# Attention and a mixture of experts on one core: experts in fixed blocks of 128 slots, shared products last

## The reference, cut to what matters

```python
xn = layernorm(x)
# attention: 16 heads of 16
scores = (q @ k.T) * SCALE * decay * causal        # no softmax
y = layernorm(scores @ v, ln_w, ln_b)
attn = (y * silu(xn @ wg.T)) @ wo.T
# experts: E = 32, K = 4, I = 192
top_vals, top_idx = top_k(xn @ router_w.T + router_b, 4)
rw = softmax(top_vals) * 1.8
routed = sum_k rw[k] * (silu(xn @ gate[e].T) * (xn @ up[e].T)) @ down[e].T
shared = (silu(xn @ sg.T) * (xn @ su.T)) @ sd.T
out = x + attn + routed + shared
```

## Time and profile before

| | us |
|---|---|
| median of 3 runs | 325.85 |
| range of the runs | 322.96 to 326.37 |
| span of the profiled execution | 308.4 |
| TensorE busy in the span | 267.0 |
| VectorE, ScalarE, GpSimd busy | 146.2, 75.3, 145.3 |

### The profile page before, as it was taken

How to read it: one execution, slowest core, us unless ns; L and a number is a source line. 1 busy time by engine, 2 the same in 40 slices (tenths; PEclk the granted TensorE clock), 3 DMA queues, 4 the chain that set the end, 5 groups by cost and what they waited for, 6 DMA issues and landing times.

```text
span 308.4 us, 5576 instructions
## 1 busy us (share of the span) xinstructions
PE 267.0 (87%) x1522; PEld 180.7 (59%) x1523; DVE 146.2 (47%) x488; ACT 75.3 (24%) x217; POOL 145.3 (47%) x164
## 2 busy tenths in 40 slices
PE   6699989998699999999999999999999999993000
PEld 2577867876488877767555565555555555551000
DVE  2913988979435563734613233223232332321393
ACT  1031231111111111211223333323333233320230
POOL 0063060607306074604375667667666676433480
PEclk9799999999699999999999999999999999998555
DMA  6999950000000002000039998984212222111982
GB/s 199 391 353 426 425 108 2 0 0 1 2 1 2 1 2 68 2 0 19 18 89 248 291 299 271 288 281 159 73 55 84 66 90 80 52 36 44 332 261 85
DMA packets 16725, 40.13 MB, mean 130 GB/s; under 512 B 2934, under 2 KB 10555, under 8 KB 16065
## 3 DMA queue, kind: packets, MB, share of 16 engines
q1 hardware_dynamic: 12048, 29.43, 28.5%
q0 software_dynamic: 4224, 9.97, 10.2%
q10 hardware_dynamic: 432, 0.47, 0.7%
HBM read 33.57 MB, written 7.86 MB: 134 GB/s over the span
## 4 chain that ended last, share of the span: by engine, by line
PE 75%; DVE 13%; DMA 4%; POOL 3%; issue 2%; ACT 0%; SPq 0%; DVEq 0%; POOLq 0%
PE bank L1110 18%; PE bank L1134 9%; PE bank L1048 8%; PE bank L1132 6%; PE bank L1102 5%; PE bank L988 4%; DVE x_sb L880 4%; PE bank L956 4%; PE bank L972 3%; PE bank L1119 3%; PE bank L964 3%; PE bank L1082 3%; DVE w L763 2%; DMA w<-y_rows 2%; PE bank L1079 2%
## 5 line engine op out<-in xcount | busy, mean ns | idle before, releaser
L1110 PE MATMUL bank<-w,xbT 128*128 x176 | 64.5, 489 | 0.6 <-ACT xbT L449 0.4
L533 POOL DMA_INDIRECT y_rows<-loop_mem,sidx x44 | 44.5, 1012 | 34.4 <-issue 25.0
L526 POOL DMA_INDIRECT xg<-xn_rows,gidx x44 | 43.1, 981 | 18.2 <-issue 12.3
L817 DVE TENSOR_TENSOR state_mem<-loop_mem,bank 128x192 f32<-128x192 f32 x44 | 15.6, 354 | 62.6 <-ACT loop_mem L453 62.6
L1110 PEld LDWEIGHTS bank<-w,xbT 128*128 128x128 f32 x176 | 30.0, 190 | 13.0 <-issue 1.2
L1048 PEld LDWEIGHTS bank<-w 128*128 128x128 f32 x256 | 31.6, 198 | 2.3 <-issue 0.6
L1048 PE MATMUL bank<-w 128*128 128x128 f32 x256 | 32.3, 281 | 0.0
L1134 PE MATMUL bank<-w,loop_mem 64*128 x88 | 30.6, 428 | 0.0
L504 POOL TENSOR_SCALAR w<-w,cst 128x256 f32<-128x256 f32 x8 | 7.8, 973 | 45.4 <-ACT w L424 45.4
L449 ACT COPY xbT<-bank 128x256 f32<-128x256 f32 x44 | 16.3, 373 | 49.6 <-PE bank L1102 49.6
L824 DVE COPY loop_mem<-bank 128x256 f32<-128x256 f32 x44 | 18.7, 425 | 20.1 <-PE bank L1134 20.1
(11 more groups left out here) (145 smaller groups left out, 385.2 us busy)
## 6 DMA issues: line engine op xcount, KB each, us to landing
w<-w_exp_dram SPq DMA_DIRECT2D x17, 512.0 KB, 5.1
w<-w_exp_dram SPq DMA_DIRECT2D x3, 2560.0 KB, 16.4
w<-y_rows SPq DMA_DIRECT2D x8, 512.0 KB, 7.3
w<-w_exp_dram SPq DMA_DIRECT2D x1, 1088.0 KB, 7.9
x_sb<-x_dram SPq DMA_DIRECT2D x4, 256.0 KB, 5.7
w<-w_qkvg_dram SPq DMA_DIRECT2D x2, 512.0 KB, 7.7
w<-decay_dram SPq DMA_DIRECT2D x1, 1024.0 KB, 10.3
xn_rows<-w SPq DMA_DIRECT2D x2, 512.0 KB, 3.4
```

Of the source, the lines that this page charges most:

```text
L526: nc.gpsimd.indirect_dma_start(xg[:, u, :], None, xn_rows, bass.IndirectOffsetOnAxis(ap=gidx[:, u:u + 1], axis=0),).then_inc(tok_in[u], 16)
L533: nc.gpsimd.indirect_dma_start(y_rows, bass.IndirectOffsetOnAxis(ap=sidx[:, w:w + 1], axis=0), ysb[:, w, :], None, bounds_check=ROWS - 1, ...
L1110: last = nc.tensor.matmul(ps_gu[(u - 1) % 2][:, 0:2 * I], xbT[:, (u - 1) % 2, g * P:(g + 1) * P], w1[:, bass.ds(e_gu * EW + g * 2 * I, 2 * ...
```

## The change

What it does, part by part:

- **Experts.** Each expert has one fixed block of 128 slots, and two experts make a pair that is worked on together in 16 steps written out without a loop. The weights are the standing operand and the tokens stream, so that the hidden values come out with features on the partitions and are not transposed. The two 64-row halves of the hidden values of a pair lie one below the other. Tokens beyond 128 go to overflow blocks of four pieces of 32 slots, each piece with an expert of its own: four such blocks are always done, more only if needed (`later_rounds`). For a piece, ScalarE copies the expert's weights (1024 columns) to a fixed place, and a small DMA brings the rest.
- **Attention.** Scores are eight products of 256 columns in four row groups. Values are weighed by 16 products that each fill 32 columns of the array, four column groups in turn. Scores of a tile are no longer cut in halves. Tile 0 is loaded and normalised alone. The state is updated one tile later. The inverse root goes over a power on GpSimd and one refinement. The query masks move to ScalarE. The output's normalisation goes over ScalarE, VectorE and GpSimd. The routing's steps lie at other tiles (ranks at 2, inverse at 6), and its one-hot positions are made by ScalarE and GpSimd.
- **Shared expert.** It leaves the attention's tiles and is done after the experts, features on the partitions, in four groups of 256 tokens. The transposed tokens are written to memory and loaded back for this.
- **Tail.** `y_rows` is ordered by partition. VectorE adds the four rows for tiles 0 to 4 and two rows of tile 5, in an order that takes two tiles in turn. TensorE adds the other ten rows by products with diagonal matrices.
- **Weights.** 9 pairs are loaded early, 7 late.

The diff's core (`...` where lines are left out):

```diff
-            def scores(t, half):
...
-                for par, q in enumerate((qe, qo)):
-                    for g in range(KT):
-                        for b in range(2):
-                            rows = slice(32 * (2 * half + b), 32 * (2 * half + b + 1))
+            def scores(t):
...
+                for g in range(KT):
+                    for r in range(HG // 2):
+                        rows = slice(CT * r, CT * (r + 1))
+                        q = qeo[rows, t % 2, :].rearrange("p (a n) -> p a n", a=2)[:, :, g * P:(g + 1) * P]
+                        last = nc.tensor.matmul(ps_s[r][:, 2 * g * P:2 * (g + 1) * P],
+                                                qk[rows, t % 2, (KT + g) * P:(KT + g + 1) * P],
+                                                q, start=True, stop=True)
...
+            def weigh_values(t):
...
+                for g in range(KT):
+                    for par in range(2):
+                        for r in range(HG // 2):
+                            s = 4 * r + 2 * g + par
+                            h = head_of_slot(s)
+                            last = nc.tensor.matmul(ps_y[CT * r:CT * (r + 1), g * P:(g + 1) * P],
+                                                    vz[:, t % 2, h * CT:(h + 1) * CT], st[:, s * P:(s + 1) * P],
...
+            def transpose_pair(p):
...
+                for j in range(2):
+                    k = AT["P", 2 * p + j]
+                    for g in range(KT):
+                        last = nc.tensor.transpose(ps_xt[p % 2][:, (2 * g + j) * P:(2 * g + j + 1) * P],
+                                                   xg[:, k % RING, g * P:(g + 1) * P], ident)
...
+            def gate_up(n):
...
+                for m in range(3):
+                    for g in range(KT):
+                        o = j * EW + g * MB + m * P
+                        last = nc.tensor.matmul(ps_gu[j][:, m * P:(m + 1) * P], w[:, o:o + P],
+                                                xbT[:, p % 2, (2 * g + j) * P:(2 * g + j + 1) * P],
...
+            def down(p):
...
+                for j in range(2):
+                    nc.tensor.matmul(ps_dn[j][:, 0:D], hA[:, 2 * (p % 2) + j, :], w[:, j * EW + KT * MB:j * EW + XW],
+                                     start=True, stop=False)
+                for j in range(2):
+                    rows = slice(j * I2, (j + 1) * I2)
+                    nc.tensor.matmul(ps_dn[j][:, 0:D], hC[rows, p % 2, :], w2[rows],
+                                     start=False, stop=True).then_inc(dn_ps, 1)
...
+            def overflow_gate_up():
+                for g in range(KT):
+                    for j in range(SUBS):
+                        rows = slice(SUB * j, SUB * (j + 1))
+                        o = j * OW + g * MB
+                        last = nc.tensor.matmul(ps_og[rows, 0:MB], xbO[:, g * P + SUB * j:g * P + SUB * (j + 1)],
+                                                o_mem[:, o:o + MB], start=(g == 0), stop=(g == KT - 1),
...
+            def shared_gate_up(i):
...
+                for m, to in enumerate((ps_sa[i % 2][:, 0:2 * P], ps_sa[i % 2][:, 2 * P:4 * P], ps_sc[i % 2][:, 0:2 * P])):
+                    for g in range(KT):
+                        o = g * MB + m * P
+                        last = nc.tensor.matmul(to, ws_mem[:, o:o + P], xnT_back[:, g, n],
...
+            def output_scale(t):
...
+                pool.wait_ge(mo_sb, t + 1)
+                step(nc.gpsimd.tensor_tensor(yrstd[:, s], yvar[:, s], minus_half[:, 0:1], ALU.pow))
...
+            def copy_weights(i, j):
+                e = act.value_load(eid_row[0:1, bass.ds(i, 1)], min_val=0, max_val=E - 1)
+                return nc.scalar.copy(o_mem[:, j * OW:j * OW + XW], w_mem[:, bass.ds(e * EW, XW)])
...
+            def weigh_routed(n):
...
+                    last = nc.tensor.matmul(ps_sd[n // 2 % 2][n % 2][:, 0:D], diag[:, i, :], back[:, n, k, :],
+                                            start=False, stop=(k == TOPK - 1 or (i, k) == rows[-1]))
```

More of the change, by code:

```diff
@@ L58 @@
 C_GC = C_KD + H
[L59 to L60 removed]
+C_IO = C_GC + KT
 C_PI = C_IO + P
@@ L319, in states_before, with state_reads @@
             return sum(1 for u in range(t) if u % CPB < CPB - 1)
+        def state_reads(t):
+            return sum(1 for u in range(t + 1) if u % CPB > 0)
         def need(eng, semaphore, value):
@@ new lines, in take_logits_transposed, with hot_positions @@
+            def take_logits_transposed():
+                act.wait_ge(lgT_ps, 1)
+                nc.scalar.copy(lgT[:, :], ps_vg[:, 0:2 * P]).then_inc(lgT_sb, 1)
+            act_hot = [a for a in range(NA) if a not in POOL_HOT]
+            hot = [0]
+            def hot_positions(t, place):
+                for _ in range(HOT_STEPS.get((t, place), 0)):
+                    a = act_hot[hot[0]]
+                    if hot[0] == 0:
+                        act.wait_ge(pos_sb, 1)
+                    nc.scalar.activation(pos_hot[:, a, :], iota_bf[:, :], ACT.Abs, scale=-1.0, bias=pos_f[:, a:a + 1]
+                                         ).then_inc(abs_sb, 1)
+                    hot[0] += 1
@@ L586, in _ @@
+            for w in range(YRING):
+                pool.wait_ge(sent[w], 16 * SENT[w])
+            later_rounds(pool, later)
         @block.vector
@@ L1162, in _ @@
+            project_qk(1)
             for t in range(NT):
                 more = t + 1 < NT
-                scores(t, 0)
+                if t >= 1:
+                    scores(t)
+                if t == CPB + 1:
+                    transpose_keys(CPB)
+                if t == 1:
+                    router_logits()
+                if t == T_INVERT:
+                    route_inverse()
+                if not more:
+                    transpose_pair(0)
+                if t % CPB > 0 and t != CPB + 1:
+                    chunk_products(t - 1)
```

1740 lines of the change are left out of this document (1109 added, 631 removed).

## The result

The changed kernel takes **235.37 us** (median of 4 runs, 235.03 to 236.57), the kernel before 325.8 us (322.96 to 326.37) beside it: a ratio of 0.7234, 95% interval 0.7193 to 0.7274. The forecast was 250 with a range of 229 to 274, so the direction and the range held and the figure was 6% too high. The profiled execution has a span of 233.7 us and a time of 235.56.

| stage | predicted | after | after, where no release is late (below) |
|---|---|---|---|
| first scores start | 14 | 11.9 | 12.0 |
| attention ends | 100.5 | 85.1 | 81.8 |
| experts | 104.2 | 124.0 | 94.4 |
| tail | 28 | 24.6 | 24.6 |
| time above the span | 17.45 | 1.9 | 1.9 |

What follows compares the result with a forecast made beforehand. The prediction took the kernel as TensorE's work plus a tail without it. Attention to 100.5, experts 104.2 and tail 28 gave a span of 232.7 us; with 17.45 carried, 250, range 229 to 274.

Steps and rivals of the forecast that it cites:

- Tiled products, taken at 2.0 times: Scores, values and overflow blocks: four row or column groups of TensorE run 2.0 times as fast, bounds 1 and 4.
- A tile of 11.5: Attention, tiles 1 to 6: TensorE 10.0 and VectorE 9.4 us, waiting for each other, take 11.5 us a tile.
- the rival in which the chain sets the attention: Attention: hand-overs between VectorE, ScalarE and GpSimd make a tile 14.5 us; +18, total 268 us, chance 0.15.
- Switches of shape: TensorE, attention and experts: each change of tiling shape is paid, 0.18 us each.
- A pair, 4.9: Expert stage: one pair of experts takes 4.9 us of TensorE, sixteen pairs 78.4 us.
- A step with overflow, 8 to 10: Expert stage: steps that include overflow work take 8 to 10 us; an overflow block costs 5.6, four 22.4.
- the slower rival: Experts' gate and up: weight loads do not hide, up to 0.19 us more per instruction; +82, 332 us, chance 0.02.
- Late weights at nothing: Expert step 4: late weights of 8.3 MB cause no wait, with 31 us of cover; if late, up to 5 us.
- The 17.45 us carried from the median of the runs: Whole kernel: the runs' median lay 17.45 us above the span before; added unchanged to the predicted span.
- The low rival: Whole kernel: all overlaps well, four groups at three times and a tile at 10; 231 us, chance 0.14.
- The column rival: Attention values and overflow: the four column groups do not overlap, values take 3.58 us again; 278 us, chance 0.12.
- The tail, 28: After the experts: TensorE 21.6 us, shared work hidden behind a tail of the old length, 28 us.

Runs made afterwards that it cites:

- a_lessshared: Changed kernel with four of six shared gate and up products left out for three of four token groups: 203.27 us, ratio 0.6552.
- a_direct: Changed kernel with the 36 gathers by index replaced by plain loads of 128 rows: 209.0 us profiled, 476.4 us in the other execution.
- b_again: The kernel before, unchanged, run again on a faster chip: 309.01 us, profile span 307.0.
- b_again2: The kernel before, unchanged, one profiled execution on a chip where the changed kernel has late releases: 323.58 us, span 321.8.
- b_values: Kernel before with only the values spread to 32 columns a head and weighed in two column groups in turn: 303.93 us, ratio 0.9806.
- a_serial: Changed kernel with the loop over the four column groups outermost in `weigh_values`: 238.44 us, ratio 0.7387.

## Why the prediction was right, and where it was not

**The bound and the order of the stages: right.** TensorE sets the attention together with VectorE, TensorE alone the experts, and the shared products fill the tail. First scores were expected at 14 and start at 11.9, within the ends of 12 and 18 but for 0.1.

**Tiled products, taken at 2.0 times: the mis-sized term.** Measured 3.2 times in four row groups, 3.5 in four column groups, and 1.43 us for 16 instructions of 384 columns in the overflow (5.15 in full rows), 3.6. I chose 2.0 since it was nearest to the one row of the trace, where two groups gave 1.6; four groups in turn come near the bound of 4. The Trainium skill, page TensorE: Matmul & The Clock Gate, section on packing small matmuls, gives 3.07 for four row groups and 2.38 for three column groups, at 512 columns. The row groups agree with it, with 3.2; for three column groups no run here has a figure, and per group the four measured are above it. My 2.0 cost 0.64 + 0.77 us a tile and 1.7 an overflow block (4.3 taken for gate, up and down, 2.6 measured), 11 + 7 us.

**A tile of 11.5: 9.3 measured.** Tiles 1 to 6 take 55.9 us, 9.3 in the mean and 7.6 to 11.3 each. Of the 2.2 us of difference, 1.4 are the term above; the rest is that the two engines wait for each other less than the 1.5 us given for it. The three tiles whose chain goes over the routing or over GpSimd reach 10.1 to 11.3 us, still short of the 14.5 of the rival in which the chain sets the attention. With tile 0 at 7.8 instead of 9.5 and the last at 9.5 instead of 8 (a late release in it), attention ends 15.4 us early.

**Switches of shape: right.** They are paid, 0.2 us each, as in L1085 above. The Trainium skill, TensorEngine Tiling (Array Packing), section Key Properties, says that a change of tiling mode drains TensorE, and the trace agrees.

**A pair, 4.9: right**, 4.76. **A step with overflow, 8 to 10: too high**, 6.3 to 6.6 where nothing is late. What its steps take beyond 4.76 adds up to 3.7 us a block, where I had 5.6. The experts would have taken 94.4 us and not 104.2: 7.6 us of the difference are the four blocks (6.9 of it their tiled products), 2.2 the sixteen pairs. The weight loads of gate and up, 204 ns in the mean, hide behind products that start 0.112 us apart, so the slower rival falls.

**Late weights at nothing: right.** In the kernel after, step 4's copies start at 115.6, in `a_lessshared`, with nothing late, at 106.5, and neither waits for them; the cover there is 33 us, from 73.0 on, where I had 31. The up to 5 us that I put on a late load are of the right size: in `a_direct` ScalarE waits 4.3 us for the weights, up to 110, and with the clock it costs TensorE 6.3 us.

**What no step had: the late releases.** They make the experts 124.0 instead of 94.4 on this chip, and the last tile some 3 us longer. The sign that I had set, TensorE busy over 95% in the loop, fails by them (105.68 of 124.00 us, against 89.53 of 90.00 in `a_lessshared`). In the trace of the kernel before I read "no idle time at all" in the loop, which is true on chips without late releases (132.04 of 133.00 us in `b_again`) and not on the others (137.79 of 146.00 in `b_again2`). Together they are 32.9 us. Against them stand the stages that I had too long: 18.7 us in the attention with the head, 9.8 in the experts, 3.4 in the tail, 31.9 in all, of which the mis-sized overlap is 18. The predicted span, 232.7 against 233.7, came out by this luck and not by its terms.

**The 17.45 us carried from the median of the runs: wrong.** I took it as something outside the span. The executions here have 1.8 to 2.2 us outside; the rest is the difference between the profile of a chip without late releases (308.4) and the runs of one with them. It should have been a part of the expert stage, to be asked about, and not a constant. With 1.9 in its place the sum would have given 234.6.

**The low rival, 231,** described the outcome best in its mechanism (four groups at three times), at a chance of 0.14, but its figure too holds the 17.45 us and no late release. The trace of the kernel before had no more to say for it than one row of two groups. The column rival is refuted: the values take 1.02 us and not 3.58, and 2.41 where the groups don't take turns.

**The tail, 28: right in its mechanism**, TensorE 21.7 (predicted 21.6), and 3.4 us too long. I put 5.4 us behind the last sum, and it is 2.1; why, no run tests.

## What to carry to other kernels

When the median of the runs lies far above the profile's span, ask which execution the profile is of before carrying the difference: it can be time inside a stage that this one execution doesn't show. Small float32 products in four row or column groups in turn ran at three times and more here (16 or 32 instructions of 128 to 384 columns), and each change of shape cost about 0.2 us. Where TensorE hands over to other engines every few microseconds, look in the waits for those without a releaser, on more than one chip, before the work itself is blamed.

## What the hardware showed that was not expected

- Waits for TensorE without a releaser, up to 7.9 us each in the kernel after and 3.9 in the kernel before. In the kernel after they begin 4 us behind the first gather by index and end at most 8 us behind the last, while scatters by index go on for another 24 us or more; in the kernel before, gathers ran from 114 us on and nothing was late before 169. The chip of `b_again`, `b_values` and `a_lessshared` is the only one that ran these gathers and shows none. Gone in the one profile in which the 36 gathers were plain loads through the same queue. Why a gather should hold up TensorE's releases, why scatters by index do not, and what differs between the chips stays open.
- At the first late release TensorE's own instructions are held up too, at full clock: in seven of the eight profiles of the changed kernel that have one, the scores L1459 take 2.06 to 2.27 us there, and 1.15 elsewhere. In the eighth, `a_serial`, they take 1.15 there too. Why stays open.
- The late releases cost some 12 us of 322 in the kernel before and about 30 of 235 in the kernel after. That it goes with how often the engines hand over is a guess; no run varies it. Without late releases the changed kernel would take about 203 us (81.8 + 94.4 + 24.6 + 1.9, put together from two profiles and not measured as such), a ratio near 0.66 to the 310 of the kernel before.
- A gather by index takes GpSimd 0.98 us to issue, a plain load of 128 rows 0.57.
- One execution of 476 us of a kernel that takes 209 in the other.
